# Attention and mixture-of-experts block on one core: two scatter-add sums for three, and a final norm shared out differently between VectorE and ScalarE

## What is computed

```python
x = x + _layernorm(_L0_attn_ref(_layernorm(x), wq, wk, wv, wo))
x = x + _layernorm(_L0_ffn_ref(_layernorm(x), router..., gate_up..., down...))
# _layernorm(x) = (x - mean) / sqrt(var + eps), over the last axis
# _L0_ffn_ref: for each row, the sum over its 4 experts of score * (down(gated(gate_up(row))) + bias)
```

## Time and profile before

| | us |
|---|---|
| median of 3 runs | 500.48 |
| lowest, highest | 499.14, 502.36 |
| the profiled execution: its time | 498.94 |
| its span | 497.0 |
| TensorE busy | 470.8 (95%) |
| VectorE, ScalarE, GpSimd busy | 361.7, 326.9, 241.8 |
| mean granted TensorE clock | 0.98 of full |

### The profile page before, as it was taken

How to read it: one execution, slowest core, us unless ns; L and a number is a source line. 1 busy time by engine, 2 the same in 40 slices (tenths; PEclk the granted TensorE clock), 3 DMA queues, 4 the chain that set the end, 5 groups by cost and what they waited for, 6 DMA issues and landing times. The chain is left out here.

```text
span 497.0 us, 11714 instructions
## 1 busy us (share of the span) xinstructions
PE 470.8 (95%) x3482; PEld 440.7 (89%) x3482; DVE 361.7 (73%) x1267; ACT 326.9 (66%) x815; POOL 241.8 (49%) x228
## 2 busy tenths in 40 slices
PE   7799999999999999999999999998599999999993
PEld 4699899999999999999999998887479999999993
DVE  3798798787875687776578798587266787876755
ACT  4878987768586777667677666575257766566612
POOL 2988884444222346445453246016635556555512
PEclk9999999999999999999999999998799999999997
DMA  8367651999500000000364355622465566566672
GB/s 255 105 207 231 215 191 60 372 369 370 175 1 1 23 26 36 24 18 33 142 237 170 128 175 218 197 61 83 67 138 91 92 98 108 93 104 101 140 192 84
DMA packets 63885, 67.49 MB, mean 136 GB/s; under 512 B 5008, under 2 KB 58704, under 8 KB 63824
## 3 DMA queue, kind: packets, MB, share of 16 engines
q1 hardware_dynamic: 55232, 55.66, 35.0%
q0 software_dynamic: 7872, 10.49, 12.2%
q10 hardware_dynamic: 720, 0.59, 0.4%
HBM read 32.63 MB, written 34.10 MB: 134 GB/s over the span
## 5 line engine op out<-in xcount | busy, mean ns | idle before, releaser
L531 POOL TENSOR_TENSOR by_sin<-by_sin,rope_sin 128x512 f32<-128x512 f32 x64 | 82.9, 1295 | 139.0 <-ACT by_sin L653 139.0
L1558 PE MATMUL bank<-xgT,gu_now 128*128 128x128 f32 x752 | 95.4, 281 | 8.3 <-issue 5.4
L1357 PE MATMUL bank<-xT_parts,qk_h 128*128 128x256 f32 x512 | 99.7, 293 | 3.6 <-DVE xT_parts L953 1.5
L1558 PEld LDWEIGHTS bank<-xgT,gu_now 128*128 128x128 f32 x752 | 90.6, 197 | 10.1 <-issue 7.6
L629 POOL DMA_INDIRECT sum_d<-y,xg x44 | 70.6, 1605 | 56.1 <-ACT y L781 49.7
L653 ACT ACTIVATE by_sin<-bank 64x512 f32<-64x512 f32 x128 | 75.8, 593 | 31.9 <-PE bank L1357 29.1
L1357 PEld LDWEIGHTS bank<-xT_parts,qk_h 128*128 128x128 f32 x512 | 79.1, 191 | 4.7 <-POOL qk_l L516 2.1
L675 ACT ACTIVATE prob<-score,row_bias 128x128 f32<-128x128 f32 (+1 forms) x128 | 57.0, 447 | 27.9 <-DVE row_bias L978 27.6
L1357 PE MATMUL bank<-xT_parts,qk_l 128*128 128x256 f32 x256 | 72.5, 283 | 0.0
L1357 PE MATMUL bank<-wv_h,xT_parts 128*128 128x256 f32 x256 | 66.6, 324 | 1.4 <-ACT V L653 1.4
L968 DVE TENSOR_TENSOR qkT<-bank,by_sin 128x512 f32<-128x512 f32 x64 | 44.3, 692 | 17.5 <-POOL by_sin L531 14.8
(11 more groups left out here) (184 smaller groups left out, 1060.1 us busy)
## 6 DMA issues: line engine op xcount, KB each, us to landing
rows_d<-blank SPq DMA_DIRECT2D x32, 576.0 KB, 7.3
gu_w<-_L_ffn_gate_up_proj_dram SPq DMA_DIRECT2D x16, 512.0 KB
xg<-rows_d SPq DMA_DIRECT2D x47, 144.0 KB
dn_w<-in_L_ffn_down_proj_dram SPq DMA_DIRECT2D x16, 256.0 KB
sum_d<-blank SPq DMA_DIRECT2D x2, 1152.0 KB, 9.8
raw_qk<-in_L_attn_wq_dram SPq DMA_DIRECT2D x16, 128.0 KB, 3.6
raw_qk<-in_L_attn_wk_dram SPq DMA_DIRECT2D x16, 128.0 KB, 3.6
raw_v<-in_L_attn_wv_dram SPq DMA_DIRECT2D x8, 256.0 KB, 2.8
```

What stands on the lines that cost most here:

```text
L531: pool.tensor_tensor(v, v, rope_sin[:, :].unsqueeze(1).broadcast_to([P, 2, T]), ALU.mult).then_inc(pool_sin, 1)
L1357: m = pe.matmul(out, lhs, rhs, start=first and i == 0, stop=last and i == len(terms) - 1, skip_group_check=not (first and last))
L1558: m = pe.matmul(ps_gu[i][:, (2 * s + r) * P:(2 * s + r + 1) * P], gu_now[:, i % 2, k, s, r * P:(r + 1) * P], xgT[:, i % XT, k, :], start=( ...
```

## The change

1. Two sums in DRAM in place of three (`SUMS` = 2). `HOME[i]` is i % 2 for all tiles, so that every add waits for the add two before it. The early read of the third sum is gone, and so is the filling of one sum with zeros. The sum of tile 42 (sum 0) is read into `sum_a`, that of tile 43 (sum 1) into `sum_b`.
2. VectorE adds the two (`add_two`), and TensorE multiplies only their sum `sum_a` with the identity. All three late tiles now go ahead of all pairs' sums.
3. ScalarE makes bank * rstd + shift from PSUM (`scale_result`), and VectorE adds x to it (`add_x`), one tile at a time. VectorE's order is: statistics of pairs 0, 1 and 2, x for pair 0, statistics of pair 3, x for pairs 1 to 3. The outputs wait for VectorE.
4. In `row_stats`, for all norms, var+eps is written and signalled ahead of -mean, which has a signal of its own (`dve_mean`), for which GpSimd waits ahead of `shift`.

```diff
-XG, XT, AR, YR, SUMS, LATE = 9, 2, 3, 6, 3, 3
+XG, XT, AR, YR, SUMS, LATE = 9, 2, 3, 6, 2, 3
...
-        TWO = LAST - 5
-        HOME = [i % SUMS if i < TWO else (TWO + (i - TWO) % 2) % SUMS for i in range(LAST)]
+        HOME = [i % SUMS for i in range(LAST)]
...
-            sp.wait_ge(dma_sum[HOME[TWO - 1]], added(TWO - 1))
-            for u in range(2):
-                sp.dma_start(sum_a[:, 4 * u:4 * u + 4, :], sum_rows[HOME[TWO - 1]][:, 4 * u:4 * u + 4, :]).then_inc(dma_first[u], 16)
-            for i, to, signal in ((LAST - 2, sum_b, dma_second), (LAST - 1, sum_c, dma_third)):
+            for i, to, signal in ((LAST - 2, sum_a, dma_first), (LAST - 1, sum_b, dma_second)):
                 sp.wait_ge(dma_sum[HOME[i]], added(i))
                 for u in range(4):
                     sp.dma_start(to[:, 2 * u:2 * u + 2, :], sum_rows[HOME[i]][:, 2 * u:2 * u + 2, :]).then_inc(signal[u], 16)
             for u in range(3):
-                sp.wait_ge(act_moe, 2 * u + 2)
+                sp.wait_ge(dve_out, 2 * u + 2)
...
                 pool.wait_ge(pool_rstd, n + 1)
+                pool.wait_ge(dve_mean, n + 1)
                 pool.tensor_tensor(shift[:, cols], minus_mean[:, cols], rstd[:, cols], ALU.mult).then_inc(pool_shift, 1)
...
-            def shift_result(u):
+            def scale_result(u):
 
                 n = NORMS.index(("moe", u))
                 sc.wait_ge(pool_shift, n + 1)
-                sc.wait_ge(dve_out, u + 1)
+                sc.wait_ge(pe_sum, u + 1)
+                sc.wait_ge(dve_two, u + 1)
                 for i in range(2):
-                    sc.activation(sum_b[:, 2 * u + i, :], sum_b[:, 2 * u + i, :], ACT.Identity,
-                                  bias=shift[:, 2 * n + i:2 * n + i + 1]).then_inc(act_moe, 1)
+                    sc.activation(sum_b[:, 2 * u + i, :], ps_sum[u][:, i * M:(i + 1) * M], ACT.Identity,
+                                  bias=shift[:, 2 * n + i:2 * n + i + 1],
+                                  scale=rstd[:, 2 * n + i:2 * n + i + 1]).then_inc(act_moe, 1)
...
-            def finish(u):
-
-                n = NORMS.index(("moe", u))
-                dve.wait_ge(pool_rstd, n + 1)
-                dve.wait_ge(act_x, u + 1)
-                for i in range(2):
-                    m = dve.scalar_tensor_tensor(out=sum_b[:, 2 * u + i, :], in0=ps_sum[u][:, i * M:(i + 1) * M],
-                                                 scalar=rstd[:, 2 * n + i:2 * n + i + 1], in1=x[:, 2 * u + i, :],
-                                                 op0=ALU.mult, op1=ALU.add)
-                m.then_inc(dve_out, 1)
+            def add_x(u):
+
+                dve.wait_ge(act_x, u + 1)
+                for i in range(2):
+                    dve.wait_ge(act_moe, 2 * u + i + 1)
+                    dve.tensor_tensor(sum_b[:, 2 * u + i, :], sum_b[:, 2 * u + i, :], x[:, 2 * u + i, :], ALU.add).then_inc(dve_out, 1)
...
+            moe_stats(0)
+            moe_stats(1)
+            moe_stats(2)
+            add_x(0)
+            moe_stats(3)
+            for u in range(1, 4):
+                add_x(u)
...
-            for j in range(LATE - 1):
+            for j in range(LATE):
                 for u in range(4):
                     add_late(u, j, first=j == 0)
             for u in range(4):
-                add_late(u, LATE - 1)
                 pe.wait_ge(dve_two, u + 1)
-                add_sum(u, sum_a)
-                pe.wait_ge(dma_third[u], 16)
-                add_sum(u, sum_c, last=True).then_inc(pe_sum, 1)
+                add_sum(u, sum_a, last=True).then_inc(pe_sum, 1)
```

More of the change, by code:

```diff
@@ L226, in block_kernel @@
         dma_sum = [sem(f"dma_sum{i}") for i in range(SUMS)]
-        dma_first = [sem(f"dma_first{u}") for u in range(2)]
+        dma_first = [sem(f"dma_first{u}") for u in range(4)]
         dma_second = [sem(f"dma_second{u}") for u in range(4)]
-        dma_third = [sem(f"dma_third{u}") for u in range(4)]
         dma_token = sem("dma_token")
@@ L270, in block_kernel @@
         dve_var = sem("dve_var")
+        dve_mean = sem("dve_mean")
         dve_xT = sem("dve_xT")
@@ L946, in row_stats @@
                 cols = slice(2 * n, 2 * n + 2)
-                dve.tensor_scalar(minus_mean[:, cols], mean_var[:, tiles, 0], -1.0, None, ALU.mult)
                 dve.tensor_scalar(var_eps[:, cols], mean_var[:, tiles, 1], EPS, None, ALU.add).then_inc(dve_var, 1)
+                dve.tensor_scalar(minus_mean[:, cols], mean_var[:, tiles, 0], -1.0, None, ALU.mult).then_inc(dve_mean, 1)
             def xT_low(b, ps):
@@ L1327, in add_two, with moe_stats @@
                 dve.tensor_tensor(sum_a[:, tiles, :], sum_a[:, tiles, :], sum_b[:, tiles, :], ALU.add).then_inc(dve_two, 1)
+            def add_x(u):
[3 more added lines that the diff above has]
+                    dve.tensor_tensor(sum_b[:, 2 * u + i, :], sum_b[:, 2 * u + i, :], x[:, 2 * u + i, :], ALU.add).then_inc(dve_out, 1)
+            def moe_stats(u):
+                dve.wait_ge(pe_sum, u + 1)
+                row_stats(ps_sum[u][:, :].rearrange("p (s m) -> p s m", s=2), "moe", u, 0)
             for u in range(4):
                 add_two(u)
-            def finish(u):
-                n = NORMS.index(("moe", u))
-                dve.wait_ge(pool_rstd, n + 1)
-                dve.wait_ge(act_x, u + 1)
-                for i in range(2):
-                    m = dve.scalar_tensor_tensor(out=sum_b[:, 2 * u + i, :], in0=ps_sum[u][:, i * M:(i + 1) * M],
-                                                 scalar=rstd[:, 2 * n + i:2 * n + i + 1], in1=x[:, 2 * u + i, :],
-                                                 op0=ALU.mult, op1=ALU.add)
-                m.then_inc(dve_out, 1)
-            for u in range(4):
-                dve.wait_ge(pe_sum, u + 1)
-                row_stats(ps_sum[u][:, :].rearrange("p (s m) -> p s m", s=2), "moe", u, 0)
-                if u:
-                    finish(u - 1)
-            finish(3)
+            moe_stats(0)
[5 more added lines that the diff above has]
+                add_x(u)
         @block.tensor
```

9 lines of the change are left out of this document (4 added, 5 removed).

## The result

| | before | after |
|---|---|---|
| median of 11 runs each, us | 500.73 | 498.56 |
| lowest, highest | 499.14, 502.36 | 497.99, 501.63 |
| ratio of the means, 95% interval | | 0.9967 (0.9952 to 0.9982) |
| the profiled execution: time, span | 498.94, 497.0 | 499.49, 497.4 |
| TensorE busy (share of the span) | 470.8 (95%) | 465.9 (94%) |

A forecast was written before the change was run, and what follows sets the result against it. TensorE was taken as the bound until 489.5 us, then a chain over four engines. -0.1 (last statistics) and -0.2 (tail) make -0.3 us: 498.6 us profiled, 500.2 us as median, range 498.6 to 501.8.

The forecast's parts named there:

- rival A: At the end, reads land early enough that VectorE isn't held at its adds: faster by some 2 us, 498.4 us; chance 0.12.
- TensorE and the new wait: At the end, four identity products fewer, but products wait for VectorE's adds: TensorE ends about 486.5 us, 3.0 us sooner.
- VectorE becomes the bound: At the end, statistics queue behind VectorE's waiting adds, losing almost all of TensorE's 3.0 us; 0.1 us is left.
- -0.1, start of the last statistics: Term for the end: pair 3's statistics begin at 489.4 us instead of 489.50, a gain of 0.1 us.
- The tail: From the last statistics to the last output's issue: 3.8 us against 3.96, a gain of 0.2 us.
- Two sums in the loop: In the tile loop, adds waiting for the add two before cost nothing: taken as 0.
- -0.2 us (less traffic): Lower bound on the effect of two sums in the loop: at best 0.2 us gained.
- Outputs: At the end, the last outputs go out closer together, at no cost; if they collide, the 0.3 us go.
- B: At the end, the last read's last quarter lands later than 484.8 us; 1 us later gives 501.2 us; chance 0.20.
- C: In the loop, adds average over 5.74 us and two sums throttle it: 507 us at 6.1 us each; chance 0.03.
- D: At the end, nothing moves: outputs, closer together, end when they did, 500.5 us; chance 0.12.

The follow-up runs named there:

- a2: The changed kernel again, unaltered, on another chip beside runs of the kernel before: 498.74 us against 499.87, ratio 0.9979.
- e1: Kernel before with parts 1 and 2 only (two sums, one identity product), old finish, shift and order: 499.76 us against 500.49, ratio 0.9981.
- e2: Kernel before with part 3 alone (ScalarE scales from the bank, VectorE adds x), three sums kept: 500.68 us, ratio 0.9998.
- e3: Changed kernel with the third sum's traffic (fill and early reads) put back, its result unused: 499.66 us, ratio 0.9981.
- f1: Kernel before, where the adds of tiles 2, 3 and 4 also wait for the add two before: 498.90 us, ratio 0.9979.
- g1: Changed kernel, first scatter-add held until tile 4's result is written, and end reordered on TensorE and VectorE: 497.25 us, ratio 0.9935.
- f3: Changed kernel with only the end reordered on TensorE and VectorE (pairs 0 and 1 first, all statistics before x): 498.90 us, ratio 0.9977.
- g3: Kernel before with one wait: first scatter-add held until tile 4's result is written; 496.71 us against 500.93, ratio 0.9927.
- h1: Changed kernel with three sums, adds held, sum 2 complete sooner, VectorE adding all sums, reordered end: 496.33 us against 500.52, ratio 0.9912.

## Why the prediction was right, and where it was wrong

The time was near: 498.56 us measured, 500.2 forecast, 498.6 to 501.8 as the range (the median lies 0.04 us under it), and the difference from before is far inside 1%, as forecast. The size of the gain was not: 0.3 us forecast, 1.0 to 1.7 measured. The cases given were the wrong ones: rival A had the size (2 us) for a reason that wasn't there.

| step | forecast | measured (after) |
|---|---|---|
| TensorE's end, us after the last add's start | 13.2 | 12.92 |
| pair 0's statistics | 11.9 | 11.48 (a2: 11.02) |
| one block of statistics | 1.16 | 1.16 |
| x for pair 0, two adds, to the next statistics | 0.73 | 0.68 |
| pair 3's statistics | 16.1 | 15.62 (a2: 15.15) |
| from there to the last output's issue | 3.8 | 4.17 (a2: 4.17) |
| last output's issue | 19.9 | 19.79 (a2: 19.32) |
| one activation from the bank | 0.55 | 0.56 |
| last row scatter to last add | as before, 126.15 | 125.18 (a2: 125.20) |

The forecast's times are taken from the last add's start in before, 473.30 us.

*TensorE and the new wait: right.* TensorE lost its eight matmuls and ended 3.25 us sooner against the last add (16.17 to 12.92). It waited for VectorE's add once, 0.3 us where 0.5 was forecast.

*VectorE becomes the bound: right,* and shown by e1: with the old, longer finish between the statistics, pair 3's begin 5.04 us after pair 0's in place of 4.14, and the end is 1.2 us later (20.96 against 19.79; the rest is e1's later reads, less its shorter tail). The first term ("-0.1, start of the last statistics") was too small by 0.5 to 0.9 us, most of it because the last reads landed sooner than the 4.6 us taken from the earlier trace rows: the third add began 10.18 us after the last scatter-add in place of 10.5, and in a2 at 9.76.

*The tail: wrong in sign.* "The tail after the statistics thus costs 3.8 us against 3.96." It costs 4.17. The working had x for pairs 1 and 2 done beside the power and counted it as free. It isn't: GpSimd's power took 0.86 us and its shift 0.43 while VectorE added two SBUF tensors, 0.69 and 0.20 otherwise (e1). That is +0.40 us, and all traces with the new tail and two sums have it (4.17 or 4.18 us in all), e2 with three sums too (0.79 and 0.44, 4.18). The Trainium skill (SBUF — State Buffer, section SBUF: two separate sides) says that a VectorE instruction with two SBUF inputs and a GpSimd instruction that reads SBUF take one port pair by turns, and that the loser waits out the other's whole instruction. The trace agrees: the shift ends at 492.18, some 0.04 us behind the end of the four adds at 492.14. Before, `finish` had one of its inputs in PSUM, and power and shift ran at full pace beside it.

The two errors at the end nearly cancel: 19.9 forecast, 19.79 measured.

*Two sums in the loop: "I take 0", wrong.* This is the step that failed. I asked only whether an add would have to wait for a sum and whether GpSimd would fall behind, and looked at the steady part. The first adds, which come in a burst behind the row scatters, I didn't look at. There the wait that two sums bring is a gain: 1.0 us from the last row scatter to the last add (126.15 to 125.18), found in every two-sum kernel that isn't held (124.69 to 125.44), without part 3 (e1) and with the old traffic (e3). f1 shows it without the two sums (124.38). The bound "-0.2 us (less traffic)" was no bound: it allowed for a gain by traffic alone.

*Part 4,* forecast at 0.07 us once, was not run alone. It is undone in e1 and e2, and a sum of this size can't be seen in them.

*Outputs: right.* The last read and write bursts hit nothing; from the last output's issue to the end of the span it takes 3.7 us (3.5 before).

*Rival A* (reads early, VectorE not held) is not what happened: VectorE was held 0.94 us before its third add and had no gap until pair 3. *B* is not seen in the two traces of the changed kernel. A late read is seen in g1: by an estimate from its issue at 6.0 us after the last add and the 5.7 us that it took, its last quarter landed about 1 us later than in the changed kernel (5.0 + 1.4 us and 4.2 us), and its last output went out 0.7 to 0.8 us later than in the changed kernel and f3. B had 1.0 us for this (501.2 against 500.2). *C* is out: one wait for a sum, 1.2 us. *D* (nothing moves) is outside the first interval (0.9952 to 0.9982), while the second (0.9958 to 1.0000) reaches it.

By these traces the 1.3 us of the two profiles are 0.97 us ahead of the last add and 0.37 us behind it; with a2 it is 0.95 and 0.84.

**What stays open.** Which step of an add holds the others up: GpSimd's issuing of it (its instruction takes 1.6 us), or the transfers behind it. The rows show only that ScalarE and VectorE start long after the matmul they wait for is recorded as ended, and the profile mostly puts the release down to "remote", so no engine of its own. Both start within 0.07 us of each other in these traces (353.87 and 353.93 in before, 350.50 and 350.56 in g3), and in the code both wait for signals of TensorE alone, which points to one event that frees them. The rows speak against the loading of code: the only transfers of instructions in this stretch of the traces begin 1.5 us or more behind the end of the stall (355.6 us in before, 352.0 in g3). Nor do I know why an execution's attention part varies by some 2 us; that is as large as the whole effect of this change.

## What to carry to other kernels

An order or a wait "that costs nothing" has to be priced at the start of a loop too, where its requests come in a burst, and not only in the steady part: here the first three scatter-adds stood in the way of TensorE's partners for over 4 us, and a single wait on GpSimd gives more than the reworked end. Where a gain of a few tenths of a percent is sought, cut both profiles at a shared event near the change; the spans of two executions differ by more than the effect. Work moved beside a chain counts as free only if no step of the chain takes longer beside it, as power and shift did here.

## What the runs showed of the hardware that I had not expected

- A scatter-add of 128 rows of 1 KB, issued by GpSimd directly behind row scatters, delays what ScalarE and VectorE wait for from TensorE, by 1.2 to 1.6 us for each (stall ends at 2.4 to 2.55, 3.92, 5.1 to 5.3 and 6.6 to 6.7 us for 0, 1, 2 and 3 adds). In the steady part, with adds some 2.9 us apart, no such stall shows.
- Reading a sum of 1 MB while adds go on holds up a late add by about 2 us: 2.18 us in before, 2.23 in e2, 2.06 in f1, 2.01 in g3, 2.57 in h1, and 1.91 in e3, where what is read is no sum at all. Neither after nor a2 has it.
- Power and shift on GpSimd took 0.86 and 0.43 us beside VectorE's adds from two SBUF tensors, 0.69 and 0.20 us without them.
